# Attention of a decoder layer: scores and value weighting each in one block, queries normalised ahead of their transposition

## The reference, cut to what matters

```python
qkv = h @ wqkv                       # h: x with half of its columns shifted by one token
q, k, v = jnp.split(qkv, 3, axis=-1)
q = l2norm(q) * qs
k = l2norm(k) * ksc
q, k = rotary_xpos(q, k)             # q * cos * scale + rotate_half(q) * sin * scale, k with 1 / scale
bq = q.reshape(b, h, w, WINDOW, d) * QK_SCALE          # 8.0
sim = jnp.einsum('bhwid,bhwjd->bhwij', bq, bk)         # bk, bv: this window and the one before
sim = jnp.where(mask, -jnp.finfo(sim.dtype).max, sim)
attn = jax.nn.softmax(sim, axis=-1)
out = jnp.einsum('bhwij,bhwjd->bhwid', attn, bv)
x = x + o @ wo
```

## Time and profile before

| | us |
|---|---|
| median of 3 runs | 1061.69 |
| lowest, highest | 1060.79, 1063.59 |
| span of the profiled execution | 1063.7 |
| PE busy | 983.9 |
| DVE busy | 697.0 |
| ACT busy | 556.5 |
| POOL busy | 398.4 |

### The profile page before, as it was taken

One profiled execution on the slowest core, in us unless ns is written; L12 is line 12 of the kernel. 1 busy time (PEld: TensorE's weight loads), 2 busy tenths in 40 slices (PEclk: granted clock), 3 DMA queues, 4 the chain that ended last, 5 costly groups with the idle time before them and its releaser, 6 DMA issues.

```text
span 1063.7 us, 18012 instructions
## 1 busy us (share of the span) xinstructions
PE 983.9 (92%) x5720; PEld 777.0 (73%) x5720; DVE 697.0 (66%) x1814; ACT 556.5 (52%) x1217; POOL 398.4 (37%) x417
## 2 busy tenths in 40 slices
PE   5889969999999979999999799998999999989987
PEld 4768855777676857777777588886777777768876
DVE  6888476366575677777778545575777777735563
ACT  4467721404030327777777734444777777754432
POOL 4232613113130366666666300115565656510030
PEclk9889979999999999999999999999999999989999
DMA  6101012000000000000001110000000000000010
GB/s 244 64 1 60 20 40 104 1 1 0 0 0 1 1 21 2 2 22 0 21 0 32 41 60 9 0 21 1 2 22 0 21 0 24 17 12 10 1 55 25
DMA packets 14349, 25.38 MB, mean 24 GB/s; under 512 B 864, under 2 KB 11224, under 8 KB 13528
## 3 DMA queue, kind: packets, MB, share of 16 engines
q1 hardware_dynamic: 14296, 24.72, 6.9%
HBM read 20.53 MB, written 2.10 MB: 21 GB/s over the span
## 4 chain that ended last, share of the span: by engine, by line
PE 74%; DVE 12%; issue 6%; ACT 4%; POOL 3%; DMA 0%; POOLq 0%; DVEq 0%; ACTq 0%
PE bank L1509 32%; PE bank L1704 5%; PE bank L1798 5%; PE bank L1656 5%; PE bank L1844 5%; PE bank L1825 4%; PE bank L1917 4%; PE bank L1810 4%; PE bank L1777 2%; PE bank L1836 2%; PE bank L1667 1%; PE bank L1784 1%; DVE scores L957 1%; POOL scanned L376 1%; PE bank L1575 1%
## 5 line engine op out<-in xcount | busy, mean ns | idle before, releaser
L1370 ACT ACTIVATE probs<-scores,row_bias,q_rnorm 128x256 f32<-128x256 f32 (+1 forms) x256 | 143.7, 565 | 10.7 <-DVE row_bias L963 10.1
L957 DVE CUSTOM_DVE_ANT_0 scores<-bank,mask 128x256 f32<-128x256 f32 (+1 forms) x256 | 89.2, 385 | 20.5 <-PE bank L1798 16.1
L507 POOL TENSOR_TENSOR norms<-norms,minus_half 128x16 f32<-128x16 f32 x32 | 93.6, 2925 | 2.7
L1509 PE MATMUL bank<-wqkv_hi,x_hi 128*128 128x512 f32 x192 | 85.4, 445 | 2.5 <-DVE rot L931 1.4
L490 POOL TENSOR_TENSOR k_tok<-rot 128x512 f32<-128x512 f32 x32 | 41.2, 1287 | 101.0 <-DVE rot L931 101.0
L1509 PE MATMUL bank<-wqkv_hi,x_lo 128*128 128x512 f32 x192 | 77.0, 401 | 0.0
L1509 PE MATMUL bank<-wqkv_lo,x_hi 128*128 128x512 f32 x192 | 77.0, 401 | 0.0
L1102 DVE SCALAR_TENSOR_TENSOR hidden<-bank,lcols,hidden 128x512 f32<-128x512 f32 (+1 forms) x48 | 35.9, 749 | 60.9 <-PE bank L1509 52.8
L1798 PE MATMUL bank<-k_t,q_t 64*128 64x256 f32 (+1 forms) x512 | 66.1, 377 | 10.1 <-DVE row_max L957 8.6
L1810 PE MATMUL bank<-ident,probs 128*128 128x128 f32 x448 | 65.9, 274 | 5.2 <-ACT probs L1370 5.0
L1342 ACT ACTIVATE squares<-bank 128x512 f32<-128x512 f32 x64 | 38.3, 598 | 61.1 <-PE bank L1509 61.1
(11 more groups left out here) (242 smaller groups left out, 2620.0 us busy)
## 6 DMA issues: line engine op xcount, KB each, us to landing
w_stage<-in_wm_l_dram SPq DMA_DIRECT2D x8, 534.0 KB, 3.5
w_stage<-in_wqkv_dram SPq DMA_DIRECT2D x2, 1536.0 KB, 7.4
out_dram<-stream SPq DMA_DIRECT2D x4, 512.0 KB, 2.9
emb<-in_ctx_dram SPq DMA_DIRECT2D x1, 1536.0 KB, 6.5
inner<-in_w_gate_dram SPq DMA_DIRECT2D x1, 1152.0 KB, 9.1
stream<-in_x_dram SPq DMA_DIRECT2D x2, 512.0 KB, 5.1
stream<-in_x_dram SPq DMA_DIRECT2D x1, 1024.0 KB, 11.5
ew<-in_pos_bias_dram SPq DMA_DIRECT2D x1, 1024.0 KB, 11.2
```

What stands on the lines that cost most here:

```text
L507: pool.tensor_tensor(norms[:, 2, :], norms[:, 1, :], minus_half[:, :], ALU.pow).then_inc(c_rn, 1)
L957: dve.tensor_tensor_reduce(scores[:, i % 2, e, 0:nk], bank[6 + e][:, (i % 2) * 2 * P:(i % 2) * 2 * P + nk], mask[:, 2 * P - nk:2 * P], 1.0 ...
L1370: act.activation(probs[:, i % 2, e, 0:nk], scores[:, i % 2, e, 0:nk], ACT.Exp, bias=row_bias[:, w % 2, h:h + 1], scale=q_rnorm[:, w, h:h + 1],
L1509: ins = pe.matmul(out, stationary, moving, start=(first and i == 0), stop=(last and i == len(terms) - 1))
```

## The change

- Queries: `rnorm` on GpSimd multiplies `q_tok` in place with the norm (128x512, after the power), instead of making `q_rnorm` (128x8). `transpose_q` waits for it (`c_rq`). The factor 8 goes into the rope tables of the queries, with a minus sign; so scores come out negated, masks add +1e30 (`FAR`) instead of -1e30, and `masked` keeps the row minimum.
- Softmax: the row minimum itself is the bias, the scale is the constant -1. The `row_bias` instruction of VectorE, four a window, and its two waits go; ScalarE waits for the masks (`c_tt`).
- Banks: `SCORES = (6, 4)`. Pairs 0 and 1 have their scores in banks 6 and 7, pairs 2 and 3 in banks 4 and 5, and the transposed probabilities of a pair go to one of the two banks of its own scores. So the scores wait for the copies of the transposed probabilities of the window before (`c_pt_out`), and a transposition for the masks of both pairs of its banks (`c_tt`).
- TensorE's order: all four pairs of scores in one block at the start of a window, then the sums, then the value weighting of all four pairs of window `n - 1` in one block (before: one half in window `n`, one in `n + 1`), then the products of queries and keys without anything between. `probs_t` gets a second half in an unused part of `w_stage` (`probs_t_far`), so that the four pairs stand side by side; the load of the second layer's `wqkv` waits for the last value weighting.
- ScalarE's order: the squares of the queries after the exponentials of pairs 0 and 1 rather than before them. VectorE's order of steps and GpSimd's stay.

```diff
@@ -200,6 +199,9 @@
         scores = sb("scores", [P, 2, 2, 2 * P], stack=st_att)
         probs = sb("probs", [P, 2, 2, 2 * P], stack=st_att)
         probs_t = sb("probs_t", [P, 2, 4, P], stack=st_att)
+        probs_t_far = w_stage[:, 2 * KD * INNER:4 * KD * INNER // 2 + 2 * 4 * P].rearrange(
+            "p (i c t) -> p i c t", i=2, t=P)
+        probs_ts = [(probs_t, probs_t_far)[i // 2][:, i % 2, :, :] for i in range(KI)]
         st_att.close()
 
         hidden = sb("hidden", [P, 2, T])
@@ -289,6 +291,8 @@
             sp.dma_start(w_2[:, :, :], w2_x).then_inc(mlp_in, 16)
 
             def load_att(l):
+                if l:
+                    sp.wait_ge(c_pv, l * NT)
                 sp.dma_start(w_stage[:, :], wqkv[l].rearrange("p k n -> p (k n)")).then_inc(wqkv_in, 16)
                 if l:
                     sp.wait_ge(c_wo, l * NT)
@@ -497,16 +501,19 @@
                 pool.tensor_copy(rsum_heads[:, :, :], row_rsum[:, :].unsqueeze(2).to_broadcast([P, HEADS, DH]))\
                     .then_inc(c_rb, 1)
 
-            def rnorm(n, w):
+            def rnorm(n, par):
 
                 pool.wait_ge(c_ss, n + 1)
                 if not (isinstance(n, int) and n == 0):
                     wait_alone(pool, c_kn, n)
+                    wait_alone(pool, c_rq, n)
                 pool.tensor_scalar(norms[:, 1, :], norms[:, 0, :], 1e-24, 1.0, ALU.max, ALU.mult).then_inc(c_clip, 1)
                 pool.wait_ge(c_clip, n + 1)
                 pool.tensor_tensor(norms[:, 2, :], norms[:, 1, :], minus_half[:, :], ALU.pow).then_inc(c_rn, 1)
                 wait_alone(pool, c_rn, n + 1)
-                pool.tensor_scalar(q_rnorm[:, w, :], norms[:, 2, 0:HEADS], QK_SCALE, 0.0, ALU.mult, ALU.add)\
+                wait_alone(pool, c_add, 2 * n + 1)
+                q = q_tok[:, par, :].rearrange("p (h d) -> p h d", d=DH)
+                pool.tensor_tensor(q, q, norms[:, 2, 0:HEADS].unsqueeze(2).to_broadcast([P, HEADS, DH]), ALU.mult)\
                     .then_inc(c_rq, 1)
 
             def split_mlp_weights(l, b, piece):
@@ -906,15 +913,17 @@
 
                 for i in range(4):
                     s = qk_scale_sb[:, l, i // 2, :].unsqueeze(1)
+                    sign = (-QK_SCALE, 1.0)[i // 2]
                     src = rope_sb[:, i, :, :]
                     dst = rope_l[:, i, :, :]
                     if i % 2:
                         for lo, other in ((0, DH // 2), (DH // 2, 0)):
-                            dve.tensor_tensor(dst[:, :, lo:lo + DH // 2], src[:, :, lo:lo + DH // 2],
-                                              s[:, :, other:other + DH // 2].to_broadcast([P, TT, DH // 2]),
-                                              ALU.mult).then_inc(c_tab, 1)
+                            dve.scalar_tensor_tensor(dst[:, :, lo:lo + DH // 2], src[:, :, lo:lo + DH // 2], sign,
+                                                     s[:, :, other:other + DH // 2].to_broadcast([P, TT, DH // 2]),
+                                                     ALU.mult, ALU.mult).then_inc(c_tab, 1)
                     else:
-                        dve.tensor_tensor(dst, src, s.to_broadcast([P, TT, DH]), ALU.mult).then_inc(c_tab, 1)
+                        dve.scalar_tensor_tensor(dst, src, sign, s.to_broadcast([P, TT, DH]), ALU.mult, ALU.mult)\
+                            .then_inc(c_tab, 1)
 
             def rope_products(n, w, i):
 
@@ -955,13 +964,9 @@
                 wait_alone(dve, c_qk, 2 * n + i // 2 + 1)
                 for e in range(2):
                     dve.tensor_tensor_reduce(scores[:, i % 2, e, 0:nk],
-                                             bank[6 + e][:, (i % 2) * 2 * P:(i % 2) * 2 * P + nk],
-                                             mask[:, 2 * P - nk:2 * P], 1.0, NEG, ALU.add, ALU.max,
-                                             row_max[:, w % 2, 2 * i + e:2 * i + e + 1]).then_inc(c_tt, 1)
-                dve.wait_ge(c_tt, 2 * u + 2)
-                dve.wait_ge(c_rq, n + 1)
-                dve.scalar_tensor_tensor(row_bias[:, w % 2, 2 * i:2 * i + 2], row_max[:, w % 2, 2 * i:2 * i + 2],
-                                         -1.0, q_rnorm[:, w, 2 * i:2 * i + 2], ALU.mult, ALU.mult).then_inc(c_nb, 1)
+                                             bank[SCORES[i // 2] + e][:, (i % 2) * 2 * P:(i % 2) * 2 * P + nk],
+                                             mask[:, 2 * P - nk:2 * P], 1.0, FAR, ALU.add, ALU.min,
+                                             row_min[:, w % 2, 2 * i + e:2 * i + e + 1]).then_inc(c_tt, 1)
 
             def invert_sums(n, w):
 
@@ -1362,28 +1367,26 @@
 
                 u = 4 * n + i
                 nk = 2 * P if w else P
-                act.wait_ge(c_nb, u + 1)
+                act.wait_ge(c_tt, 2 * u + 2)
                 if not (isinstance(n, int) and n == 0 and i < 2):
                     act.wait_ge(c_pt, u - 1)
                 for e in range(2):
                     h = 2 * i + e
                     act.activation(probs[:, i % 2, e, 0:nk], scores[:, i % 2, e, 0:nk], ACT.Exp,
-                                   bias=row_bias[:, w % 2, h:h + 1], scale=q_rnorm[:, w, h:h + 1],
+                                   bias=row_min[:, w % 2, h:h + 1], scale=-1.0,
                                    accum_out=row_sum[:, w % 2, h:h + 1]).then_inc(c_ex, 1)
 
             def probs_transposed(n, w, i):
 
                 u = 4 * n + i
+                src = bank[SCORES[i // 2] + i % 2][:, :].rearrange("p (c t) -> p c t", t=P)
                 act.wait_ge(c_pt, u + 1)
-                if not (isinstance(n, int) and n == 0 and i < 2):
-                    act.wait_ge(c_pv, 2 * n + i // 2)
+                if not (isinstance(n, int) and n == 0):
+                    act.wait_ge(c_pv, n)
                 if w:
-                    act.activation(probs_t[:, i % 2, :, :], bank[4 + i % 2][:, :].rearrange("p (c t) -> p c t", t=P),
-                                   ACT.Copy).then_inc(c_pt_out, 1)
+                    act.activation(probs_ts[i], src, ACT.Copy).then_inc(c_pt_out, 1)
                 else:
-                    act.activation(probs_t[:, i % 2, 0:4:2, :],
-                                   bank[4 + i % 2][:, :].rearrange("p (c t) -> p c t", t=P)[:, 0:4:2, :],
-                                   ACT.Copy).then_inc(c_pt_out, 1)
+                    act.activation(probs_ts[i][:, 0:4:2, :], src[:, 0:4:2, :], ACT.Copy).then_inc(c_pt_out, 1)
 
             def sums_transposed(n):
 
@@ -1394,11 +1397,10 @@
             def window(n, w, l, prev, one, two, three):
                 if prev:
                     sums_transposed(n - 1)
-                if two:
-                    square(n + 2, 0)
                 exps(n, w, 0)
                 exps(n, w, 1)
                 if two:
+                    square(n + 2, 0)
                     square(n + 2, 1)
                 probs_transposed(n, w, 0)
                 probs_transposed(n, w, 1)
@@ -1780,51 +1782,50 @@
             def transpose_q(n, par):
 
                 pe.wait_ge(c_kt, n + 1)
+                pe.wait_ge(c_rq, n + 1)
                 for c in range(KI):
                     ins = pe.transpose(bank[2][:, c * P:(c + 1) * P], q_tok[:, par, c * P:(c + 1) * P], ident[:, :])
                 ins.then_inc(c_t, 1)
 
-            def score_pairs(n, w, g):
-
-                if g == 0:
-                    pe.wait_ge(c_qt, n + 1)
-                if not (isinstance(n, int) and n == 0 and g == 0):
-                    pe.wait_ge(c_tt, 8 * n + 4 * g)
+            def score_pairs(n, w):
+
+                pe.wait_ge(c_qt, n + 1)
                 k0 = max(w - 1, 0) * P
                 nk = (w + 1) * P - k0
-                for i in (2 * g, 2 * g + 1):
+                for i in range(KI):
+                    if i % 2 == 0 and not (isinstance(n, int) and n == 0):
+                        pe.wait_ge(c_pt_out, 4 * n - 2 + i)
                     for e in range(2):
                         half = slice(e * DH, (e + 1) * DH)
-                        ins = pe.matmul(bank[6 + e][:, (i % 2) * 2 * P:(i % 2) * 2 * P + nk], q_t[half, i, :],
-                                        k_t[half, i, k0:(w + 1) * P], start=True, stop=True)
-                ins.then_inc(c_qk, 1)
+                        ins = pe.matmul(bank[SCORES[i // 2] + e][:, (i % 2) * 2 * P:(i % 2) * 2 * P + nk],
+                                        q_t[half, i, :], k_t[half, i, k0:(w + 1) * P], start=True, stop=True)
+                    if i % 2:
+                        ins.then_inc(c_qk, 1)
 
             def transpose_probs(n, w, i):
 
                 u = 4 * n + i
                 pe.wait_ge(c_ex, 2 * u + 2)
-                if not (isinstance(n, int) and n == 0 and i < 2):
-                    pe.wait_ge(c_pt_out, u - 1)
+                pe.wait_ge(c_tt, 8 * n + 4 * (i // 2) + 4)
                 for e in range(2):
                     for k in range(2 if w else 1):
```

(25 more changed lines are left out.)

21 lines of the change are left out of this document (10 added, 11 removed).

## The result

The changed kernel takes 1106.51 us (median of 4 runs, 1105.5 to 1108.03) against 1062.12 for the kernel before (4 runs beside them): ratio 1.042, 95% interval 1.040 to 1.043. It is slower by 44 us, where 37 were forecast (1099, range 1080 to 1115). The profiled execution took 1105.5 us, its span is 1103.7. It was the fastest of its four and the one profiled before the slowest of its four, so the two spans lie 40 us apart and not 44.

The account below looks back on a forecast made before the run. It took TensorE's program order to bound the repeated windows, with new waits on VectorE and ScalarE chains after the change. 24 windows x 1.8 = +43 us, edges -6, so +37 on 1061.69: 1099 us, range 1080 to 1115.

Parts of the forecast that it names:

- TensorE is the bound of the repeated windows before, and not after: Repeated attention windows: TensorE's program order set the time before; afterwards it waits and is busy about 86%.
- Three changes of tile shape fewer: TensorE in a window: seven shape changes become four, about 0.17 us each, worth 0.5 us (0.3 to 0.8).
- O waits 0.6, K 1.0, S 0.6: TensorE waits: output projection 0.6 us for o_t, key transposition 1.0 for the residual, scores' second half 0.6 for banks.
- the key norm: VectorE step between o_t and the masks: masked scores start 0.81 us after it.
- The sum: Full attention window added up from the engines' chains: 15.6 us against 13.89 before.
- The bound for it, 0.3 us a window: GpSimd's new query product: cost 0, at most 0.3 us a window through VectorE's key norm beside a busier GpSimd.
- The edges: Eight attention windows outside the 24 repeated ones: -3 us a layer (0 to -5), -6 in all.
- The softmax part, costed at nothing: Softmax terms cost 0; exponentials 0.085 us shorter each, 0.7 us a window of ScalarE, worth 0.
- GpSimd's product of the queries costs nothing: GpSimd's 128x512 query multiplication replaces a 128x8 step: cost 0, since GpSimd has 3.8 us free a window.
- The clock rival: New TensorE gaps in attention windows lower the clock: 24 x 1 us more, about 1125 us; chance 0.06.

Follow-up runs that it names:

- all orders with four changes: The changed kernel (1106.51 us) and two reorderings of it that keep scores and value weighting in one block each and cover the waits (1053.76 and 1052.92 us).
- the softmax part alone: Kernel before with only the change's softmax and query edits, keeping before's banks and TensorE and ScalarE orders: 1052.82 us, ratio 0.992.
- everything but TensorE's order: Changed kernel with scores and value weighting in halves in before's places, and ScalarE's query squares in before's place: 1052.35 us, ratio 0.990.
- the run with W between Mq and Mk: Changed kernel with value weighting moved between the query and key products, and ScalarE's query squares ahead of the first exponentials: 1077.84 us, ratio 1.014.

## Why the prediction was right, and where it was off

- **TensorE is the bound of the repeated windows before, and not after.** Right: 87% busy (86% forecast), clock 1.00.
- **Three changes of tile shape fewer are worth 0.5 us a window.** Right in size: the work and the switches come to 13.4 in all orders with four changes, where 16.1 - 2.7, 13.71 - 0.35 and 13.6 - 0.25 agree. The rule of the Trainium skill, that a change of mode drains the engine (TensorEngine Tiling (Array Packing), section Tiling Modes), agrees with the rows: 0.33 us from start to start at a change, 0.25 or less without. The gain of 0.5 was less than the cover it was bought with.
- **O waits 0.6, K 1.0, S 0.6.** Found: 0.65, 1.4 and 0.7, with the releasers that were named. Each was moved on its own: K's by VectorE's order (-0.46), S's by ScalarE's (-0.48), O's and K's by TensorE's (-1.2).
- **The term that was mis-sized is the key norm.** The sum took 0.81 us from its start to the first mask out of a window in which the norm started ahead of GpSimd's rope sum; in the new order it starts 0.35 behind it, and the step is 1.38. The kernel before has this too: in the first of the twelve windows the norm starts 0.34 us behind the sum and takes 1.49. The bound for it, 0.3 us a window, was set under the head of GpSimd's new product, and was too small: the neighbour was the old rope sum. With the norm's overlap gone the window is 15.67, where the sum said 15.6; that the two agree is in part luck, since the step is then 0.60 and not 0.81, and the residual waits for O. Over the 24 windows the overlap is worth 8.5 us.
- **The edges.** Forecast -6; in the spans they came to -11, with a further -2.4 ahead of the first scores. The prediction says that the last three windows have no Mq or Mk; window 13 has both, and grew from 13.2 to 14.6 us in each layer, so the others gave -14. The softmax part, costed at nothing, is one source: I costed the shorter exponential only in the full windows, where it is hidden, and not in the windows where TensorE waits for VectorE and ScalarE, which the prediction itself had named. The higher clock of the changed kernel's profiled execution is another; their shares stay open. In the spans, the repeated windows were put 10 us too low (53 against 43) and the rest 7 too high. The errors have opposite signs, so the total came out closer than its parts, which is luck.
- **GpSimd's product of the queries costs nothing.** Right: the softmax part alone, which has it, takes 1052.8 against 1062 with full windows no longer than before, and the product takes 1.04 us.
- **The clock rival.** It didn't come in the windows. At the end of the first layer's attention the clock went the other way; the stretches around the last output projection before, and the like after (stretch, PE busy, clock):

```profile
602.80:607.80 5.00, 2.85 (x24) 0.97 0.02 5
607.80:612.80 5.00, 4.16 (x22) 0.50 0.71 263
```

```profile
627.50:632.50 5.00, 3.21 (x40) 1.00 0.02 5
632.50:637.50 5.00, 4.53 (x20) 1.00 0.84 313
```

The last O takes 3.2 us before and 1.6 after. Before, TensorE did 2.85 of 5.0 us of work ahead of the slow stretch; after, it did 3.21 of 5.0 and stayed at the higher level. The Trainium skill (TensorE: Matmul & The Clock Gate, section HAM oscillation) lets one expect a lower clock behind gaps; the trace of before doesn't contradict it. The change can't be called the cause: from 600 to 670 us the clock was 0.95 in the run of everything but TensorE's order, and 1.00 in that of the softmax part alone.

## What to carry to other kernels

When a block of work on the busy engine is moved, count what it covered: add up, from the trace, the other engines' chain from the block ahead of the gap to the one behind it, and compare it with the matmuls that are left between them. Here 5.5 us were left for 7.1 to 7.5 of chain, and no saving of a half us on TensorE could pay for that. Cost a shortened instruction in every stage it occurs in, and ahead of all in those where the bound engine already waits; and look at which neighbour an instruction will have in the new order, and which of the two will start first, not only at its duration in the old.

## What the runs showed of the hardware

- A VectorE multiplication of two operands in SBUF (128x512, the key norm) takes 0.68 us beside an idle GpSimd. Where a GpSimd instruction was running already when it started, it ended about 0.55 us after that one (0.49 to 0.62 in all such cases of the traces): the GpSimd instruction had 0.35 us left in the window of before and the norm took 0.90; it had 0.77 left in one of the softmax part alone (1.32), 0.91 in the changed kernel (1.47) and 1.18 in a window of the run with W between Mq and Mk (1.74). Where the GpSimd instruction started second, that one was lengthened and the norm was not: at 503 us of the softmax part alone, GpSimd's product for the split weights started 0.10 behind the norm and took 1.38 instead of 0.95, the norm 0.68; the rope sum of before, 1.73 instead of 1.26, is the same case. The profile's spans of GpSimd are rough, and no experiment varied the order of the two alone. `o_t`, 128x512 with one operand in PSUM, took 0.68 beside GpSimd's work too.
- GpSimd's 128x512 product with a norm that is broadcast along 64 columns takes 1.04 us, less than its sum of two full operands (1.28).
- The exponential of 128x256 (with row sums) takes 93 ns less if its scale is a constant and not an operand: 471 against 564 ns in the mean. The Trainium skill (ScalarE: Activation LUTs, section What ACT_TABLE_LOAD costs) puts a per-partition pointer operand at about 93 ns; the two runs agree.
